# Graph attention and mixture of experts on one core: a gather ring of 40 items in place of 36, and edge targets broadcast as 8-bit integers

## The reference

```python
def reference(x, src, dst, edge_attr_16, edge_attr_4, W_n, attn_l, attn_r, attn_m, router_w, w1, w2, w3):
    # 6250 nodes x 256, 200000 edges sorted by dst; 8 heads of 32, 4 edge types
    feat = (layernorm(x) @ W_n).reshape(N, 8, 32)
    el, er = einsum('nhd,hdt->nht', feat, attn_l), einsum('nhd,hdt->nht', feat, attn_r)
    em = einsum('ef,hft->eht', edge_attr_16, attn_m)
    e = (einsum('eht,et->eh', el[src] + er[dst] + em, edge_attr_4)) / 3.0
    e = where(e > 0, e, 0.2 * e)
    a = segment_softmax(e, dst)                       # over the edges of one target
    x = x + segment_sum(feat[src] * a[:, :, None], dst)
    # then a top-2 mixture of 8 experts (256 -> 682 -> 256, silu(h1) * h3) on layernorm(x)
    return x + moe(layernorm(x))
```

## Time and profile before

| | |
|---|---|
| time, 3 runs | 3997.48 us median (3990.64 to 3997.62) |
| the profiled execution | 3993.91 us, span 3992.3 us, mean granted TensorE clock 0.804 |
| edge loop in it | first gather 265.9 us, last add 2851.1 us |
| busy over the span | PE 74%, DVE 49%, POOL 48%, ACT 41% |

### The profile page before, as it was taken

One profiled execution on the slowest core, in us unless ns is written; L12 is line 12 of the kernel. 1 busy time (PEld: TensorE's weight loads), 2 busy tenths in 40 slices (PEclk: granted clock), 3 DMA queues, 4 the chain that ended last, 5 costly groups with the idle time before them and its releaser, 6 DMA issues. The chain is left out here.

```text
span 3992.3 us, 58396 instructions
## 1 busy us (share of the span) xinstructions
PE 2961.9 (74%) x12566; PEld 2280.4 (57%) x12567; DVE 1951.3 (49%) x5344; ACT 1636.8 (41%) x3684; POOL 1906.2 (48%) x1988
## 2 busy tenths in 40 slices
PE   4523777766777767777777677777665999999997
PEld 3223666555565655555655555556553777777775
DVE  6612565655555665566665555656771222222221
ACT  4522555444545445454554444544432222222221
POOL 2224666666666666666666666666073111111111
PEclk9755777887777888788778778877755999999998
DMA  9753444444445445544444444448554122221223
GB/s 286 239 168 104 132 135 134 134 134 132 134 134 144 127 129 140 141 135 133 133 135 134 132 135 133 134 135 119 129 190 164 32 32 32 31 32 31 32 32 84
DMA packets 304910, 481.43 MB, mean 121 GB/s; under 512 B 162103, under 2 KB 231427, under 8 KB 295854
## 3 DMA queue, kind: packets, MB, share of 16 engines
q0 software_dynamic: 105760, 312.03, 30.8%
q1 hardware_dynamic: 185486, 155.19, 13.1%
q10 hardware_dynamic: 13392, 11.23, 1.0%
HBM read 408.52 MB, written 76.12 MB: 121 GB/s over the span
## 5 line engine op out<-in xcount | busy, mean ns | idle before, releaser
L834 POOL DMA_INDIRECT rows<-table,idx x1664 | 1578.3, 948 | 981.0 <-issue 457.0
L877 PE MATMUL ps_acc<-rows,hot 128*128 128x264 f32 x3328 | 1214.0, 496 | 314.6 <-issue 150.8
L877 PEld LDWEIGHTS ps_acc<-rows,hot 128*128 128x128 f32 x3328 | 716.0, 238 | 418.9 <-issue 304.3
L862 PEld LDWEIGHTS ps_term<-er,hot_t 128*128 128x128 f32 x3328 | 607.4, 239 | 227.5 <-issue 164.2
L862 PE MATMUL ps_term<-er,hot_t 128*128 x3328 | 566.9, 300 | 99.8 <-issue 75.2
L1166 DVE TENSOR_TENSOR rows<-rows,ps_p 128x512 f32<-128x512 f32 x832 | 566.0, 680 | 6.0 <-ACT ps_p L986 0.5
L975 ACT ACTIVATE hot<-iota_row,neg_rel 128x128 f32<-128x128 f32 x1664 | 545.7, 388 | 14.3 <-PE ps_acc L877 11.6
L1749 PE MATMUL ps_h<-w,acc 128*128 x1680 | 528.5, 457 | 0.5 <-ACT acc L1668 0.5
L1661 POOL DMA_INDIRECT x_dram<-acc,to x105 | 161.8, 1541 | 760.2 <-ACT acc L1677 760.2
L1182 DVE TENSOR_TENSOR acc<-acc,ps_acc 128x264 f32 x832 | 354.9, 427 | 317.4 <-issue 173.7
L958 ACT ACTIVATE hot_t<-dst_row,neg_part 128x1024 f32<-128x1024 bf16 x208 | 235.7, 1133 | 497.6 <-remote 386.1
(11 more groups left out here) (269 smaller groups left out, 2860.5 us busy)
## 6 DMA issues: line engine op xcount, KB each, us to landing
dst_row<-rel_d SPq DMA_DIRECT2D x52, 1024.0 KB
rows<-table,idx POOLq DMA_INDIRECT x1664
rec<-rec_d SPq DMA_DIRECT2D x832, 24.0 KB
rec_d<-acc POOLq DMA_DIRECT2D x16, 1050.0 KB, 8.4
acc<-slots_x SPq DMA_DIRECT2D x105, 130.0 KB, 2.1
acc<-in_edge_attr_dram SPq DMA_DIRECT2D x16, 700.0 KB
wrow<-in_L_ffn_w_dram ACTq DMA_DIRECT2D x16, 640.0 KB
table<-fo POOLq DMA_DIRECT2D x49, 148.0 KB, 8.0
```

What stands on the lines that cost most here:

```text
L834: pool.indirect_dma_start(rows[:, in_ring(k) + j, :], None, table, bass.IndirectOffsetOnAxis(ap=idx[w][:, t:t + 1], axis=0)).then_inc(gath ...
L862: last = pe.matmul(ps_term[s % 2][:, t * HT:(t + 1) * HT], hot_t[s % 2][:, t, :], flat(er[:, ds(b, 1), :]), start=False, stop=(t == QT - 1))
L877: last = pe.matmul(ps_acc[(k1 - 1) % SUM_BANKS][:, 0:PW], hot[m // QI % 2][:, m % QI * G + j, :], rows[:, in_ring(i * (2 * NI) + at) + j, ...
```

## The change

The ring holds 40 items; the lags stay. `rel_d`, `rel_b` and `dst_row` become 8-bit unsigned integers (they hold 0 to 128), so the broadcast writes 4096 bytes a partition and not 8192. `prep_f` shrinks to the 64 columns that are used, and its transpose to 64 output rows. The ring's 9472 bytes a partition more come from these and from `zero_row`, which is now made in the router stage.

```diff
-ROW_ITEMS = 36
+ROW_ITEMS = 40
-    rel_d = [dram(f"rel_d{w}", (NI * ITEM,), BF16) for w in range(2)]
+    rel_d = [dram(f"rel_d{w}", (NI * ITEM,), U8) for w in range(2)]
-        zero_row = sb(ctx, "zero_row", [P, DIM])
...
-                    pool.memset(zero_row[:, :], 0.0).then_inc(consts, 1)
...
-                    pe.wait_ge(consts, 5)
+                    pe.wait_ge(consts, 4)
...
-            prep_f = [sb(st, f"prep_f{w}", [P, P]) for w in range(2)]
-            rel_b = sb(st, "rel_b", [BT, P], BF16)
+            prep_f = [sb(st, f"prep_f{w}", [P, 2 * BT]) for w in range(2)]
+            rel_b = sb(st, "rel_b", [BT, P], U8)
-            dst_row = [sb(st, f"dst_row{w}", [P, BT, P], BF16) for w in range(2)]
+            dst_row = [sb(st, f"dst_row{w}", [P, BT, P], U8) for w in range(2)]
...
-                        pe.transpose(prep_at, prep_f[w][:, :], ident[:, :]).then_inc(prep_ps, 1)
+                        pe.transpose(prep_at[0:2 * BT, :], prep_f[w][:, :], ident[:, :]).then_inc(prep_ps, 1)
...
+                    pool.memset(zero_row[:, :], 0.0).then_inc(r_const, 1)
...
+                    sp.wait_ge(r_const, 8)
                     sp.dma_start(x2_dram[ROWS:ROWS + P, :], zero_row[:, :]).then_inc(dummy_out, 16)
-                    sp.wait_ge(r_const, 7)
...
-                    dve.wait_ge(r_const, 7)
+                    dve.wait_ge(r_const, 8)
```

More of the change, by code:

```diff
@@ L14 @@
 I32 = mybir.dt.int32
-BF16 = mybir.dt.bfloat16
+U8 = mybir.dt.uint8
 ALU = mybir.AluOpType
@@ L1260, in gnn_moe_kernel @@
             pad = sb(st, "pad", [P, RW])
+            zero_row = sb(st, "zero_row", [P, DIM])
             pad_row = sb(st, "pad_row", [1, EXPERTS], I32)
```

## The result

The median of 20 runs is 4005.89 us (3991.65 to 4030.07), that of the kernel before in 20 runs 3990.15 us (3977.45 to 4006.7). The ratio is 1.0035, with a 95% interval of 1.0018 to 1.0051: slower, by 14 us, where I had forecast no change that can be measured. The profiled execution took 4006.02 us.

The account below looks back on a forecast made before the run. The prediction took the loop to be bound by waits and the pace of queues, with no engine near full. From the profiled 3993.9 us, +5 (start), -3 (end) and -6 (broadcast) gave 3990 us, range 3966 to 4006.

Parts of the forecast that it names:

- What bounds the kernel: Edge loop: no engine near full, waits and queue pace bind it; the ring holds POOL back, POOL doesn't hold the readers.
- The start: Loop start: eight added gathers slow SP's record loads and delay the third broadcast; +5 us, bounds 0 and +10.
- The steady loop: Mid-loop: four items of extra ring depth leave runs and gaps unchanged, since nobody waits for earlier rows; 0 us.
- Rival 2: Steady loop: the deeper ring lengthens runs of gathers, leaving fewer gaps a batch; -44 us, 3946 us, chance 0.10.
- The end: Loop end: gathers four items earlier remove the last quad's 3.02 us wait for rows; -3 us, bounds 0 and -5.
- The small parts: Fewer pieces on ACT, smaller transpose, store and fills count nothing; the router's `zero_row` fill delays DVE by at most 0.3 us.
- The 8-bit targets: Broadcasts in the loop land 1.4 us earlier, 8-bit reads cost nothing more; -6 us, bounds 0 and -21.
- gains it once for each spell: ACT's waits for the broadcast come in some five spells of batches, each gaining 1.4 us once: 7 us.
- Rival 1: Broadcast: the earlier landing counts at each of ACT's 15 waits; -21 us, 3970 us in all, chance 0.16.
- rival 4: Broadcast takes as long with 4096 bytes a partition as with 8192; 3996 us, no change; chance 0.52 together with the forecast.
- Rival 3: Loop start: the added gathers' whole 10.0 us goes through, broadcast and end gain nothing; 4004 us, slower, chance 0.16.
- my likeliest case: Whole kernel: 3983 to 3999 us, nearly all within the 0.2% that a measurement can't tell from no change.

Follow-up runs that it names:

- the sweep: Changed kernel with POOL's item k waiting for the sums of k - 28, 32, 36, 38 or 40: 1.0754, 1.0027, 1.0001, 1.0009 and 1.0035 of the kernel before.
- the two pairs: Traces of the kernel before and the changed kernel: first 3993.9 and 4006.02 us; then both again on one chip, the kernel before at 4028.99 us, ratio 1.0034.
- Start36: Changed kernel with items 36 to 39 alone held until the sums of item k - 36, later items waiting for k - 40: 1.0029 of the kernel before.
- after_again: The changed kernel once more, unaltered, on the same chip as a repeat of the kernel before: 1.0034 of the kernel before.
- pool_slower_1: 8-bit targets with a ring of 36, plus a 256-byte fill on POOL ahead of each item's gathers: 0.9983 of the kernel before.
- stop_per_8: Changed kernel with one wait of POOL for eight items in place of one for each item: 1.1722 of the kernel before, 62.97 us a batch.
- early40: Changed kernel waiting for k - 40 in the first 11 batches and k - 36 after, on a chip without interference: 1.0002 of the kernel before.
- lag28_place40: Changed kernel with place for 40 items, but item k waits for the sums of item k - 28: 1.0754 of the kernel before.

## Why the prediction was wrong, point by point

**What bounds the kernel** was read half right. That no reader waits for rows in the steady loop is shown by the sweep: 32, 36, 38 and 40 have batches of the same length within 0.2 us, 28 has not. (The lead is smaller than the "two or three quads" of the prediction: in the kernel before, a quad's L1102 begins 19.6 us in the median, 14.5 at least, after its last gather has ended, and a quad takes 12.) What I called "bound by waits and by the pace of queues" hides an effect that I had in the rows for SP alone and did not look for elsewhere: beside runs of gathers DVE, ACT and PE are held as well. Where it is absent the same kernel takes 3525 us.

**The start**: +5 forecast, bounds 0 and 10. It measured 8: the release by the first sum is 8.2 us later between the two pairs' means (142.8 and 134.6 us after the first gather). That the number lies inside the bounds is in part luck, since the path was wrong. The step that failed is "These gathers are in nobody's way on POOL, but SP loads its records then": it let the added gathers overlap with the work of DVE, ACT and PE at no cost. SP's loads and the third broadcast are late as forecast (9.8 us, and 11.8), but they are not on the way to the first sum. DVE's `less` is: DVE stood 8.83 us before it and not 1.18, the last 7.7 of them with PE's result there. Of the 9.6 us by which the third batch's compare is late, 7.8 are ACT's own delay behind this; the late broadcast adds 1.7 (ACT waits 2.03 us for it and not 0.30). Start36 shows that holding items 36 to 39 back doesn't avoid the cost: the four items of lead are paid for whenever POOL gathers them.

**The steady loop**: "I therefore cost the steady loop at 0". Between the pairs it differs by 5 and 3 us over 40 batches when a batch is taken from its first L1102, and by 5.6 and 0.4 when it is taken from its first `add`; single traces with one depth differ as much. A cost there is not shown. Rival 2, the ring buys pace, was wrong: POOL stops for more than 1.5 us 163 times before and 163 times after, and runs of 12 gathers went from 37 to 21.

**The end**: -3 forecast, -4.3 and -3.4 measured between the pairs from the start of batch 50. Right, the wait of 3.02 us is gone.

**The small parts**: as forecast. The fill of `zero_row` delays DVE's first step of the router by 0.25 us, and its wait for `xg` right behind is 0.15 shorter than in the earlier trace rows:

```profile
2866.59 0.21 DVE L1479 TENSOR_SCALAR inv<-acc 128x56 f32<-128x56 f32 x1 [1.26 <-POOL not_above L1319]
...
2872.24 2.02 DVE L1485 TENSOR_TENSOR xg<-xg,acc 128x1792 f32<-128x1792 f32 x1 [2.84 <-DMA xg<-in_x_dram]
```

**The 8-bit targets**: -6 forecast, 0 measured (1.0002, bounds -4 and +6 us), and this is the term that the sum had most wrong. The price was right: 3.8 us from issue to waiting reader in after_again (one case is 1531.97 to 1535.74) against 5.1, and L956 at 1131 ns. What failed is "gains it once for each spell": that ACT's waits for the broadcast stand for time of the loop. They don't. In the changed kernel's trace there are 3 and no longer 15, and the batch stayed at 48.3 to 48.4 us; in pool_slower_1 3 and not 37, at 0.9983. Why a landing 1.4 us sooner gains nothing, no run shows. Rival 1 (-21) falls with it, rival 4 (no shorter broadcast) too.

Summed from the first gather to the last add, the first pair differs by 8.2 to the release, 3.3 to batch 10, 4.8 to batch 50 and -4.3 at the end, 12.0 us; the second by 8.2, 0.3, 2.8 and -3.4, 7.9 us. The ratio says 14 (7 to 20). Only the start and the end agree in both pairs, 4 to 5 us together; where the rest of the 14 falls is not shown. (Outside the loop the first pair differs by 0.4 us: the router is 2.8 longer and the rest shorter. Two traces of the kernel before have 214.5 and 221.0 us in the router.) Rival 3, slower through the start, named the sign and the place; I gave it 0.16 because I let -6 and -3 stand against it. That the measured 4005.89 still lies within my range is luck: the range was made wide for rivals, and my likeliest case said that nothing would be measured.

## What to carry to other kernels

When engines that share no data all start again at one moment, look for what they have in common before pricing any of them. In the kernel before, 202 waits of DVE and ACT of over 2 us are put down to "remote", and 150 of them end 1.5 to 3.2 us after the last gather of a run of POOL. In this kernel the ring had a best depth: every further item was paid for once, when it was gathered ahead, and given back only in part at the end; sweep it both ways. Count a wait in more than one trace of the same kernel before you price it (here 15 and 37), and follow the late step back from what it releases, since the first late transfer need not be on its path.

## What the runs showed of the hardware

- Beside long runs of gathers on POOL the other engines are held back, under one of two conditions. With it: 16 record loads of SP in 61 to 68 us beside gathers; of SP's 5491 steps in the loop of the kernel before, 1218 begin 0.6 to 0.8 us after the one ahead has ended, 852 us in all; PE, DVE and ACT silent for 7.5 us (stop_per_8); 202 waits of DVE and ACT of over 2 us named "remote"; a loop of 48.3 to 49.2 us a batch. Without it, in early40: 17.1 us, no such step of SP, no such wait, 40.0 us a batch, by the same instructions of the same length (a gather 946 ns, 948 in the kernel before). The chips of the comparison above and three more showed it (3990 to 4038 us for the kernel before), two did not (3525), and one chip number stands in both lists, so that I can't say whether it is the chip, its host or what else runs there. Its cause is open.
- The bar of a gather is not its transfer. By the Trainium skill, page "Perfetto Trace Analysis", section "DMA Instruction — SWDGE (GPSIMD)", a software DMA ends in the profile when its descriptors are made, not when the data has moved. The traces agree: in early40 the bar of a gather is 0.95 us, and where DVE waits for a quad's rows its L1100 begins 2.07 us (median of 193) after the quad's last bar has ended; in lag28_place40, whose expectation put this landing at 1.6, it is 2.04 (199).
- One wait for eight items in place of eight waits made the kernel 17% slower; one for four items 0.9%, under the condition with interference. Without it three waits a batch cost nothing (1.0004).
- A bf16 and an 8-bit source cost ACT the same, 1133 and 1131 ns for 128x1024.
